# A ViT layer's window attention: one row maximum over both halves of a group, then the two subtractions

## The reference, cut to what matters

```
attn = softmax(q * scale @ k^T, axis=-1)      # 64 keys per row
out  = (attn @ v)                             # back to rasters, then proj
h    = out @ proj_w.T + proj_b
h    = h + scan(layernorm(h));  h = h + experts(layernorm(h))
```

## Time and profile before

| | us |
|---|---|
| median of 3 runs | 610.61 (608.54 to 611.0) |
| the profiled execution, its time | 610.79 |
| the profiled execution, span from first to last instruction | 609.0 |
| PE busy in the span | 541.0 (89%) |
| DVE busy in the span | 493.6 (81%) |
| ACT busy in the span | 403.9 (66%) |
| POOL busy in the span | 349.8 (57%) |
| attention, first reduction to last | 57.8 to 278.2 |

### The profile page before, as it was taken

One profiled execution on the slowest core, in us unless ns is written; L12 is line 12 of the kernel. 1 busy time (PEld: TensorE's weight loads), 2 busy tenths in 40 slices (PEclk: granted clock), 3 DMA queues, 4 the chain that ended last, 5 costly groups with the idle time before them and its releaser, 6 DMA issues. The chain is left out here.

```text
span 609.0 us, 18377 instructions
## 1 busy us (share of the span) xinstructions
PE 541.0 (89%) x7273; PEld 391.1 (64%) x7274; DVE 493.6 (81%) x911; ACT 403.9 (66%) x723; POOL 349.8 (57%) x388
## 2 busy tenths in 40 slices
PE   5797999999999999999557676759999999999996
PEld 4797889999988899998212232435555555555553
DVE  4887688888888888885798999858888888888873
ACT  3575788888888888889596676325454545454543
POOL 8303367777779877774799499653333333333320
PEclk9898799999999999999797889869999999999999
DMA  9732222222222222210000000000010101111111
GB/s 193 111 43 46 55 59 64 56 61 59 57 61 58 56 62 59 55 44 10 1 0 0 0 1 1 3 2 18 18 28 20 26 21 25 22 23 23 24 23 27
DMA packets 62382, 23.06 MB, mean 38 GB/s; under 512 B 45780, under 2 KB 62292, under 8 KB 62292
## 3 DMA queue, kind: packets, MB, share of 16 engines
q1 hardware_dynamic: 61200, 21.63, 17.5%
q10 hardware_dynamic: 964, 0.20, 0.2%
q0 software_dynamic: 128, 0.00, 0.0%
HBM read 5.02 MB, written 4.19 MB: 15 GB/s over the span
## 5 line engine op out<-in xcount | busy, mean ns | idle before, releaser
L762 DVE TENSOR_REDUCE work<-psum 128x16 f32<-128x1024 f32 x64 | 78.0, 1220 | 31.6 <-PE psum L597 31.6
L697 ACT ACTIVATE work<-work 128x1024 f32<-128x1024 f32 x64 | 67.8, 1060 | 23.1 <-DVE work L767 23.1
L767 DVE TENSOR_TENSOR work<-psum,work 128x1024 f32<-128x1024 f32 x64 | 78.4, 1225 | 2.2
L705 ACT ACTIVATE work<-psum 128x512 f32<-128x512 f32 x128 | 70.9, 619 | 3.1 <-PE psum L612 2.2
L612 PE MATMUL psum<-kc,work 128*128 128x128 f32 x512 | 68.6, 278 | 3.2 <-ACT work L697 2.8
L1681 POOL TENSOR_TENSOR m_rstd<-m_var,m_mhalf 128x4 f32<-128x4 f32 x32 | 32.2, 1008 | 61.9 <-DVE m_var L1889 61.9
L628 PEld LDWEIGHTS psum<-work 128*64 128x64 f32 x2048 | 62.3, 138 | 5.4 <-issue 5.1
L628 PE MATMUL psum<-work 128*64 128x18 f32 x2048 | 65.5, 212 | 0.0
L612 PEld LDWEIGHTS psum<-kc,work 128*128 128x128 f32 x512 | 59.8, 143 | 7.5 <-ACT work L697 2.9
L1704 PE MATMUL psum<-x_t,w1x 64*64 64x256 f32 x1024 | 64.4, 390 | 0.0
L484 POOL TENSOR_TENSOR work<-work,kc 128x512 f32<-128x512 f32 x32 | 41.9, 1309 | 38.5 <-DMA work<-big_bc 26.8
(11 more groups left out here) (198 smaller groups left out, 1281.2 us busy)
## 6 DMA issues: line engine op xcount, KB each, us to landing
work<-big_bc SPq DMA_DIRECT2D x256, 32.0 KB, 2.0
h_all<-in_x SPq DMA_DIRECT2D x16, 256.0 KB, 5.3
work<-big_a SPq DMA_DIRECT2D x32, 128.0 KB, 2.2
out<-out_st SPq DMA_DIRECT2D x126, 32.0 KB
w1x<-in_L_ffn_W SPq DMA_DIRECT2D x2, 128.0 KB, 4.2
kc<-constants SPq DMA_DIRECT2D x1, 202.0 KB, 2.8
w2x<-in_L_ffn_W SPq DMA_DIRECT2D x1, 128.0 KB, 3.5
work<-in_L_tok_qkv_w ACTq DMA_DIRECT2D x2, 32.0 KB, 3.5
```

The source lines that it names most:

```text
L697: act.activation(prob[:, f], prob[:, f], ACT.Exp).then_inc(prob_done, 1)
L705: act.activation(prob_t[:, f, 4 * half:4 * half + 4, :].rearrange("p j q -> p (j q)"), banks[4 + half][:, :], ACT.Copy).then_inc(prob_t_do ...
L762: dve.tensor_reduce(top[:, f, :].rearrange("p (g h) -> p g h", g=4), sc, AX.X, ALU.max).then_inc(top_done, 1)
L767: dve.tensor_tensor(prob[:, f].rearrange("p (g h) k -> p g h k", g=4), sc, top[:, f, :].rearrange("p (g h) -> p g h", g=4).unsqueeze(3).br ...
```

## The change

`lower` is called once per step, not twice. The reduction now takes the 2048 scores of both halves in one instruction (its input and output get one more dimension, f), `top_done` counts one per group, and behind it come the subtraction of half 0 and that of half 1. The subtractions have the same operands, waits and semaphore as before. Nothing on another engine is edited.

```
-        def lower(i, f):
+        def lower(i):
-            sc = psum[:, 0:4, f * 256:f * 256 + 256].rearrange("p g (h k) -> p g h k", k=WIN)
+            sc = psum[:, 0:4, :].rearrange("p g (f h k) -> p f g h k", f=2, k=WIN)
             dve.wait_ge(scores_done, i * 4 + 4)
-            dve.tensor_reduce(top[:, f, :].rearrange("p (g h) -> p g h", g=4), sc, AX.X, ALU.max).then_inc(top_done, 1)
-            dve.wait_ge(top_done, i * 2 + (f + 1))
-            if not first(i):
-                dve.wait_ge(turned, i * 4 + (2 * f - 2))
-            dve.tensor_tensor(prob[:, f]..., sc, top[:, f, :]..., ALU.subtract).then_inc(low_done, 1)
+            dve.tensor_reduce(top[:, :, :].rearrange("p f (g h) -> p f g h", g=4), sc, AX.X, ALU.max
+                              ).then_inc(top_done, 1)
+            dve.wait_ge(top_done, i + 1)
+            for f in range(2):
+                if not first(i):
+                    dve.wait_ge(turned, i * 4 + (2 * f - 2))
+                dve.tensor_tensor(prob[:, f]..., sc[:, f], top[:, f, :]..., ALU.subtract).then_inc(low_done, 1)
...
-                lower(i + 1, 0)
-                lower(i + 1, 1)
+                lower(i + 1)
```

More of the change, by code:

```diff
@@ L757, in run_dve @@
     def run_dve(dve, ahead):
-        def lower(i, f):
-            sc = psum[:, 0:4, f * 256:f * 256 + 256].rearrange("p g (h k) -> p g h k", k=WIN)
+        def lower(i):
+            sc = psum[:, 0:4, :].rearrange("p g (f h k) -> p f g h k", f=2, k=WIN)
             dve.wait_ge(scores_done, i * 4 + 4)
-            dve.tensor_reduce(top[:, f, :].rearrange("p (g h) -> p g h", g=4), sc, AX.X, ALU.max).then_inc(top_done, 1)
-            dve.wait_ge(top_done, i * 2 + (f + 1))
-            if not first(i):
-                dve.wait_ge(turned, i * 4 + (2 * f - 2))
-            dve.tensor_tensor(prob[:, f].rearrange("p (g h) k -> p g h k", g=4), sc,
-                              top[:, f, :].rearrange("p (g h) -> p g h", g=4).unsqueeze(3).broadcast_to([P, 4, 4, WIN]),
-                              ALU.subtract).then_inc(low_done, 1)
+            dve.tensor_reduce(top[:, :, :].rearrange("p f (g h) -> p f g h", g=4), sc, AX.X, ALU.max
[4 more added lines that the diff above has]
+                    dve.wait_ge(turned, i * 4 + (2 * f - 2))
+                dve.tensor_tensor(prob[:, f].rearrange("p (g h) k -> p g h k", g=4), sc[:, f],
+                                  top[:, f, :].rearrange("p (g h) -> p g h", g=4).unsqueeze(3).broadcast_to([P, 4, 4, WIN]),
+                                  ALU.subtract).then_inc(low_done, 1)
         def normalise(i):
```

## The result

The changed kernel takes 620.67 us (median of 4 runs, 619.72 to 621.25) against 610.04 before (4 runs): 1.0174 times as long, with a 95% interval of 1.0157 to 1.0191. The forecast was 625.8 with a range of 620.5 to 631.5: the direction and the mechanism were right, the loss was 10.6 us and not 15.

A forecast was written before the change was run, and what follows sets the result against it. TensorE bounds the stage, with the chain through the copy of the values close behind; steps go from 6.98 to 7.45 us. 1.08 + 0.41 + 12.95 + 0.61 = 15.05 on 610.79 gives 625.8 us, range 620.5 to 631.5.

The forecast's parts named there:

- The chain: Per step: scores, maximum, subtraction, exp, copy of the values, turn, next scores; about 0.4 us to spare before the change.
- transposes to next scores: TensorE: next scores start 0.58 us after the waiting second four transposes, read from an early step.
- The reduction, 2.30 us: VectorE: one reduction of 2048 elements takes 2.30 us, with bounds of 2.29 and 2.44.
- The rival with a dear form: VectorE: the longer reduction takes 2.44 us or more, or runs as two passes; step 7.59, time 630; chance 0.03.
- From exp to copy, 1.08 us: ScalarE: the copy of the values starts 1.08 us after the start of the exp of half 0.
- The sum: Whole kernel: group 1 1.08, group 2 0.41, 29 steps 12.95, last group 0.61; together 15.05 us.
- The last group, 0.61: Hand-over to the scan: exp of half 1 is 0.61 us later, passed on because ScalarE is busy 2.78 of 3.00 us.
- Exp of half 0 just in time, at no cost: ScalarE to TensorE: exp ends at 111.92, TensorE wants it at 111.96; cost about nothing.
- The room of some 0.4 us for the copy: Before the change, the chain through ScalarE's copy of the values to TensorE's turn has about 0.4 us to spare.
- The rival that fewer instructions pay: The later subtraction sets the pace and comes 0.16 us sooner per step: 5.1 us gained, 605.7 us; chance 0.03.
- The rival that nothing changes: The lateness is hidden, TensorE reaching its second four transposes at 112.8 or later; 610.8 us; chance 0.05.
- The clock: Idle of about 0.4 us per TensorE step lowers the clock; step 12.5 us, time near 790; chance 0.02.

The follow-up runs named there:

- the shorter copy: Changed kernel with the two copies of the values cut from 256 to 64 columns each, leaving out three quarters of the values: 612.35 us, 1.0048 times before.
- the table of offsets: Exp-of-half-0 start after scores against step: before 3.83/6.98; 2, 3, 4 small ScalarE copies added to it 4.39/6.98, 4.74/7.14, 5.08/7.47; two reductions first 4.84/7.24; changed 4.90/7.31 us.

## Why the prediction was right in kind and nearly half again too large

In the profiled executions the loss is 10.5 us, where 15.05 was predicted. Of the 4.55 us between them, 3.93 lie in the 29 steady steps, 0.14 in group 2, 0.46 in the last group and what follows it, and 0.02 in group 1. Against the median the forecast is off by 5.1 us, since it started from 610.79, and the kernel before has its median at 610.04.

The chain was named link by link, so that each can be laid beside the changed kernel's step.

| link | predicted, us | measured, us |
|---|---|---|
| scores to reduction | 1.32 | 1.32 |
| reduction to first subtraction | 2.34 | 2.32 |
| subtraction to exp | 1.25 | 1.26 |
| exp to copy of the values | 1.08 | 0.96 |
| the copy | 0.82 | 0.81 |
| copy to transposes | 0.06 | 0.05 |
| transposes to next scores | 0.58 | 0.59 |
| the step | 7.45 | 7.31 |

- *The reduction, 2.30 us*: 2.292. The line through 256 and 1024 elements held at 2048, also with one more dimension. The rival with a dear form is out.
- *From exp to copy, 1.08 us*: this is the term that was mis-sized, and it makes 0.12 of the 0.14 us per step. It was read from the very first group. The changed kernel has 1.08 there too, but 0.96 in each of the 31 groups behind it; the timeline of its ScalarE shows both:

```profile
61.47 1.06 ACT L697 ACTIVATE work<-work 128x1024 f32<-128x1024 f32 x1 [5.83 <-DVE work L768]
62.55 0.82 ACT L716 ACTIVATE work<-psum 64x256 f32<-64x256 f32 x2
...
70.29 1.06 ACT L697 ACTIVATE work<-work 128x1024 f32<-128x1024 f32 x1 [1.33 <-DVE work L768]
71.26 0.80 ACT L716 ACTIVATE work<-psum 64x256 f32<-64x256 f32 x2
```

  In the earlier trace rows the copy waited for the values, so that the steady steps of before could not show this spacing; one row of a start-up step stood for all. The bounds took in the reduction and the transposes but not this link, which had been held for known; so the measured step lies below the lowest one that was allowed for, 7.35. That the time still fell into the range, by 0.17 us, is luck in part: its lower end was widened for the start and for the hand-over to the scan, not for this.
- *The sum*: 29 steps gave 9.02 and not 12.95. The first group gave 1.06 (1.08 predicted), the second 0.27 (0.41, the same link again).
- *The last group, 0.61*: the exp of half 1 is in fact 0.46 later there (291.51 less 286.14, against 280.68 less 275.77), but the stage's end was tied to TensorE's 0.33, not to ScalarE: from the last group's reduction to a VectorE instruction of the scan it is 311.90 - 286.14 = 25.76 against 301.21 - 275.77 = 25.44 before. Some 0.2 us came back in what follows. "Passed on by a busy engine" was the step that failed: ScalarE was busy, but still waited for the turned u, in both kernels. Its copy (line 734) starts 0.04 us after TensorE has turned it, before (the first two rows) and after (the last two):

```profile
283.06 0.38 PE L652 MATMUL psum<-kc,work 128*128 128x128 f32 x2
...
283.48 0.39 ACT L734 ACTIVATE u_all<-psum 128x256 f32<-128x256 f32 x1
```

```profile
293.75 0.38 PE L652 MATMUL psum<-kc,work 128*128 128x128 f32 x2
...
294.17 0.38 ACT L734 ACTIVATE u_all<-psum 128x256 f32<-128x256 f32 x1
```

- *Exp of half 0 just in time, at no cost*: half right. The working set the exp's end, 111.92, against the start of the transposes' matmuls, 111.96, and found it 0.04 us early. But it is their weight loads that wait, and these start at 111.75 before the change; in the changed kernel they wait 0.25 us for the exp. While the copy's wait stands behind it, this costs nothing; the shorter copy laid it bare as the next limit, a step of 7.04 in place of 6.98.
- *The room of some 0.4 us for the copy*: by the table of offsets the exp may start at 4.58, so the copy 0.96 later at 5.54. Before, it stood at 5.19 (111.14 - 105.95 in the earlier trace rows), held by the values: a room of 0.35 us. This held.
- *The rival that fewer instructions pay*: VectorE's saving is real, 5.5 us over the span, 0.17 us for each of the 32 instructions fewer, and nothing of it reaches the time. By the Trainium skill (VectorE: DVE Perf Modes, Rules for kernel authors) the number of chained operations is what to reduce; here the trace agrees on the fixed part of each and disagrees on the result.
- *The rival that nothing changes*: by the Trainium skill (Perfetto Trace Analysis, Identifying the Most-Contended Engine) the fullest engine is the one to look at, and TensorE is to be judged by its weight loads and not by how long matmuls are busy. By either it was TensorE: its weight loads are busy for 184.11 of 205.00 us, ScalarE for 177.83. No work of it was changed; but its instructions wait in order, and the changed engine's first result is what one of them waits for. TensorE's busy time in the stretch is 210.57 of 212.12 us, and the step is longer all the same, since that count hides waits: the eight transposes of half 0 stand as one row of 1.36 us (107.97), where they stood as 1.04, with the 0.29 us wait of the weight loads inside it. The weight loads show it: 179.44 of 212.12 us, 85%, where they were busy for 90%.
- *The clock*: 1.00 from 74.02 to 286.14; no part of the loss.

## What to carry to other kernels

Two pairs of dependent operations in a pipeline (maximum, subtraction, maximum, subtraction) give their first result after one pair; merged or regrouped they give it after almost both, and what is saved in instructions is paid where somebody waits for the first result. Ask of a merge who takes the first half's result, what is queued behind that one in its own stream, and how much room the bound engine has left at that point. When working such a chain out, take each spacing from a steady step, and where the steady steps hide it behind a wait, keep both ends of it in the range.

## What the runs showed of the hardware

- On ScalarE, from the start of an exp of 1024 elements (1.06 us long) to that of the copy behind it there are two spacings: 0.96 us for the copy of the values in steady steps, which starts before the exp has ended, and 1.08 or 1.09 us for the same copy in the first group and for the copies of turned data behind the exp of half 1 (113.26 - 112.17 in the earlier trace rows). Both have waits that were long met. Why they differ was not found.
- On VectorE a reduction of 2048 elements through four PSUM banks, in four free dimensions, takes 2.292 us, in line with 1.219 for 1024. The start of a dependent operation comes 1.26 us after that of a reduction of 1024 (108.53 - 107.27 in the earlier trace rows), that of an independent one 1.14 after a subtraction.
